# Five blocks of x loaded ahead instead of seven, and the last eight tiles scaled on GpSimd in a graph-attention kernel

## What is computed

```python
def reference(x, adj, key, value, Wq, bq, Wk, bk, Wv, bv, Wm, bm):
    q, k, v = x @ Wq.T + bq, key @ Wk.T + bk, value @ Wv.T + bv
    scores = einsum('nd,md->nm', q, k) / sqrt(4096) * adj
    scores = where(abs(scores) < 1e-5, -1e9, scores)
    y = x + einsum('nm,md->nd', softmax(scores), v) @ Wm.T + bm
    return (y - mean(y)) / sqrt(var(y) + 1e-5)        # over the last axis
```

## Time and profile before

| what | value |
|---|---|
| median of 3 runs | 447.91 us (447.75 to 448.69) |
| profiled execution, its own time | 449.37 us |
| its span, first to last instruction | 447.6 us |
| PE busy | 432.1 us (97%) |
| DVE busy | 315.8 us (71%) |
| ACT busy | 190.3 us (43%) |
| POOL busy | 168.7 us (38%) |
| mean granted PE clock | 0.990 of 2.4 GHz |
| DMA | 121.58 MB, 272 GB/s in the mean |

### The profile page before, as it was taken

The page is one execution under the profiler, slowest core; times in us unless marked ns, Lnnn a source line. Parts: engine busy times, 40 slices in busy tenths (PEclk is TensorE's granted clock), DMA queues, the critical chain, the costliest instruction groups (busy, mean ns, idle before and its releaser), DMA issues.

```text
span 447.6 us, 5475 instructions
## 1 busy us (share of the span) xinstructions
PE 432.1 (97%) x1536; PEld 245.7 (55%) x1536; DVE 315.8 (71%) x923; ACT 190.3 (43%) x448; POOL 168.7 (38%) x180
## 2 busy tenths in 40 slices
PE   8999999899999999999999999999999999999982
PEld 5344444344444456566666666666566656666651
DVE  0347525698439647787888889888879878847675
ACT  1233422323333243434445454554545445464573
POOL 3100000000425118463655656547205776174300
PEclk9999999989999999999999999999999999999997
DMA  8999999999999999987899999999949879568333
GB/s 324 369 236 276 294 287 288 227 244 240 284 321 331 343 307 257 299 306 234 252 299 261 325 317 326 339 346 304 299 169 302 256 227 364 168 187 292 108 142 115
DMA packets 32452, 121.58 MB, mean 272 GB/s; under 512 B 5080, under 2 KB 5336, under 8 KB 30370
## 3 DMA queue, kind: packets, MB, share of 16 engines
q0 software_dynamic: 16240, 72.79, 61.1%
q1 hardware_dynamic: 12866, 28.51, 17.6%
q10 hardware_dynamic: 3312, 19.89, 11.3%
HBM read 139.78 MB, written 17.56 MB: 352 GB/s over the span
## 4 chain that ended last, share of the span: by engine, by line
PE 76%; issue 10%; DMA 6%; DVE 4%; ACT 3%; POOL 1%; POOLq 0%; DVEq 0%; ACTq 0%
PE bank L574 24%; PE bank L564 14%; PE bank L682 12%; PE bank L720 12%; PE bank L664 6%; DMA big<-adj_tiles 6%; PE bank L615 3%; PE bank L693 2%; PE bank L673 2%; PE bank L608 1%; ACT keyT L893 1%; ACT y_buf L951 1%; DVE stats L1277 1%; POOL big L462 1%; DVE big L1057 1%
## 5 line engine op out<-in xcount | busy, mean ns | idle before, releaser
L574 PE MATMUL bank<-big,M 128*128 128x472 f32 (+1 forms) x288 | 121.9, 550 | 0.3 <-ACT y_buf L838 0.3
L564 PE MATMUL bank<-y_buf,big 128*128 128x512 f32 x256 | 113.3, 602 | 0.7 <-ACT y_buf L860 0.7
L481 POOL DMA_INDIRECT v_g<-table,index x70 | 71.9, 1027 | 80.8 <-PE bank L720 51.9
L471 POOL DMA_INDIRECT key_adj_g<-key_adj,index x70 | 73.3, 1046 | 49.7 <-DVE index L1145 29.0
L564 PEld LDWEIGHTS bank<-y_buf,big 128*128 128x128 f32 x256 | 48.7, 192 | 60.5 <-issue 59.0
L574 PEld LDWEIGHTS bank<-big,M 128*128 128x128 f32 x288 | 51.9, 190 | 46.0 <-issue 43.8
L1057 DVE TENSOR_TENSOR big<-big 128x1888 bf16<-128x1888 bf16 x35 | 39.8, 1137 | 52.9 <-DMA big<-adj_tiles 52.9
L682 PE MATMUL bank<-keyT,qT 128*118 128x256 f32 x280 | 66.3, 380 | 0.7 <-ACT keyT L893 0.7
L462 POOL DMA_DIRECT2D big<-adj_tiles x35 | 19.9, 568 | 124.5 <-PE bank L564 82.0
L720 PE MATMUL bank<-v_g,probT 128*118 128x512 f32 x136 | 64.0, 593 | 0.5 <-ACT probT L930 0.5
L682 PEld LDWEIGHTS bank<-keyT,qT 128*118 128x118 f32 x280 | 50.8, 182 | 22.6 <-issue 10.9
(11 more groups left out here) (122 smaller groups left out, 469.8 us busy)
## 6 DMA issues: line engine op xcount, KB each, us to landing
big<-adj_tiles POOLq DMA_DIRECT2D x35, 944.0 KB, 14.6
x_buf<-x SPq DMA_DIRECT2D x35, 256.0 KB, 7.4
out<-y_buf SPq DMA_DIRECT2D x34, 256.0 KB, 5.5
big<-valueT ACTq DMA_DIRECT2D x8, 1024.0 KB, 11.3
big<-xT SPq DMA_DIRECT2D x7, 944.0 KB, 10.6
table<-qT ACTq DMA_DIRECT2D x5, 1024.0 KB, 14.6
table<-y_buf ACTq DMA_DIRECT2D x3, 1024.0 KB, 16.0
big<-xT ACTq DMA_DIRECT2D x2, 944.0 KB, 8.6
```

Of the source, the lines that this page charges most:

```text
L471: pool.indirect_dma_start(key_adj_g[:, b, c, :], None, key_adj, bass.IndirectOffsetOnAxis(index[:, t, CH + c:CH + c + 1], 0),).then_inc(ke ...
L481: pool.indirect_dma_start(v_g[:, b, c, :], None, table, bass.IndirectOffsetOnAxis(index[:, t, c:c + 1], 0), bounds_check=N - 1, oob_is_err ...
L564: mm = nc.tensor.matmul(bank[4 + t % 2][:, :], col_buf[nb % 2][:, d, k * P:(k + 1) * P], G[:, d, :], start=(d == 0), stop=(d == DC - 1))
L574: mm = nc.tensor.matmul(ps[:, 0:n], M[:, d, a * P:(a + 1) * P], xT_buf[nb % 2][:, d, 0:n], start=(d == 0), stop=(d == DC - 1))
```

## The change

Five blocks of x are loaded ahead of the loop instead of seven; the other two follow inside the loop, behind the load of xT. Tiles 26 to 33 (`LATE`) are scaled by POOL, behind its last gather, instead of by ACT; their stores come last in SP's order. The roots of 31 and 32 (step 34) and of 33 (step 35) are refined by seven short operations each on POOL instead of four for all three on DVE. ACT takes the roots of 31 and 32 ahead of `copy_prob(34)`. The keys of tile 34 are copied in two parts with `sizes(33)` between them. `add_x(32)` moves behind the first operation of `soften(34)`. The four fillers before the last `prob_transposes` are removed.

```diff
+XAHEAD = 5
...
-            last = {T - 3: [T - 7, T - 6, T - 5], T - 1: [T - 4, T - 3, T - 2], T: [T - 1]}
+            last = {T - 3: [T - 7, T - 6, T - 5], T - 1: [T - 4, T - 3], T: [T - 2], T + 1: [T - 1]}
...
+        LATE = range(T - 9, T - 1)
...
-            if i == T:
-                return [T - 2, T - 1]
-            if i == T - 3:
-                return sqrt_of(i - 2)[2:]
-            if i >= T - 2:
-                ready = sqrt_of(T - 3)
-                return ready[:2] if i == T - 2 else ready[2:] + sqrt_of(i)[:2]
+            if i > T - 4:
+                return []
...
-            for t in range(XB):
+            for t in range(XAHEAD):
                 load_x(t)
...
-                if i >= 1 and i + XB - 1 < T:
-                    load_x(i + XB - 1)
-            store(T - 2)
+                if i + XAHEAD < T:
+                    load_x(i + XAHEAD)
+            for t in LATE:
+                store(t)
...
+            def finish(t):
+                y = y_buf[0:R, t % YB, :]
+                nc.gpsimd.tensor_scalar(y, y, rstd[0:R, t:t + 1], shift[0:R, t:t + 1], ALU.mult, ALU.add).then_inc(late_fin, 1)
+
+            def scales(i, ts):
+                a, b = ts[0], ts[-1] + 1
+                n = i - (T - 1)
+                near, step = std[0:R, a:b], shift[0:R, a:b]
+                pool.wait_ge(std_sb, roots_before(i) + 1)
+                nc.gpsimd.tensor_scalar(step, mean_var[0:R, a:b, 1], EPS, None, ALU.add).then_inc(late_step, 1)
+                pool.wait_ge(late_step, 4 * n + 1)
...
+                nc.gpsimd.tensor_tensor(rstd[0:R, a:b], step, near, ALU.mult).then_inc(late_rstd, 1)
...
+            for t in LATE:
+                if t < T - 4:
+                    pool.wait_ge(shift_sb, scaling_of(t))
+                if t in (T - 4, T - 2):
+                    i = T - 1 if t == T - 4 else T
+                    scales(i, sqrt_of(i))
+                finish(t)
...
-                if i == T - 1:
-                    keep_clock(4)
...
                 if i < T:
+                    if i == T - 2:
+                        copy_keys(i + 1, range(1))
                     sizes(i)
-                    if i == T - 1:
-                        finish(late.pop(0))
-                    if LAST_QUERY < i < T - 1:
+                    if i == T - 2:
+                        copy_keys(i + 1, range(1, CH))
+                    elif LAST_QUERY < i < T - 2:
                         copy_keys(i + 1)
...
-                if i < T - 1 and sqrt_of(i):
+                if sqrt_of(i):
                     roots(i, sqrt_of(i))
...
+            roots(T + 1, sqrt_of(T + 1))
+            finish_half(T - 1)
...
                 if t < T - 1:
                     key_bias(t + 1)
+                else:
+                    add_x(t - 2)
...
                 for t in values_of(i):
-                    add_x(t)
+                    if t != T - 3:
+                        add_x(t)
...
-                if sqrt_of(i):
+                if i < T - 1 and sqrt_of(i):
                     scales(i, sqrt_of(i))
                 if i == T:
+                    scales(T + 1, sqrt_of(T + 1))
```

More of the change, by code:

```diff
@@ L251, in build @@
         fin_sb = sem("fin_sb")
+        late_fin = sem("late_fin")
+        late_step = sem("late_step")
+        late_rstd = sem("late_rstd")
+        late_shift = sem("late_shift")
         last_sb = sem("last_sb")
@@ L376, in scaling_of @@
         def scaling_of(t):
-            return next(roots_before(i + 1) for i in range(T + 1) if t in sqrt_of(i))
+            return next(roots_before(i + 1) for i in range(T + 2) if t in sqrt_of(i))
         def scores_of(t):
@@ L416, in store @@
             def store(t):
-                sp.wait_ge(fin_sb, t + 1)
+                if t in LATE:
+                    sp.wait_ge(late_fin, LATE.index(t) + 1)
+                else:
+                    sp.wait_ge(fin_sb, t + 1)
                 sp.dma_start(out_tiles[t], y_buf[:, t % YB, :]).then_inc(stored[t % YB], 16)
@@ L524, in _ @@
                     gather_keys(i + KD)
+            def finish(t):
[8 more added lines that the diff above has]
+                pool.wait_ge(late_step, 4 * n + 1)
+                nc.gpsimd.tensor_tensor(step, step, near, ALU.mult).then_inc(late_step, 1)
+                pool.wait_ge(late_step, 4 * n + 2)
+                nc.gpsimd.tensor_tensor(step, step, near, ALU.mult).then_inc(late_step, 1)
+                pool.wait_ge(late_step, 4 * n + 3)
+                nc.gpsimd.tensor_scalar(step, step, -0.5, 1.5, ALU.mult, ALU.add).then_inc(late_step, 1)
+                pool.wait_ge(late_step, 4 * n + 4)
+                nc.gpsimd.tensor_tensor(rstd[0:R, a:b], step, near, ALU.mult).then_inc(late_rstd, 1)
+                pool.wait_ge(late_rstd, n + 1)
+                nc.gpsimd.tensor_tensor(step, mean_var[0:R, a:b, 0], rstd[0:R, a:b], ALU.mult).then_inc(late_shift, 1)
+                pool.wait_ge(late_shift, 2 * n + 1)
+                nc.gpsimd.tensor_scalar(step, step, -1.0, None, ALU.mult).then_inc(late_shift, 1)
+                pool.wait_ge(late_shift, 2 * n + 2)
+            for t in LATE:
[5 more added lines that the diff above has]
+                finish(t)
             with overflow(pool) as n:
@@ L886, in copy_q, with copy_keys @@
                                      ).then_inc(q_sb, 1)
-            def copy_keys(t):
+            def copy_keys(t, chunks=range(CH)):
                 if t >= 1:
@@ L891, in copy_keys @@
                 act.wait_ge(keyT_adjT_ps, t + 1)
-                for c in range(CH):
+                for c in chunks:
                     nc.scalar.activation(keyT[:, :, c * P:(c + 1) * P],
@@ L942, in finish_half @@
                 y = y_buf[0:R, t % YB, 0:HD]
-                act.wait_ge(shift_sb, scaling_of(t))
+                act.wait_ge(shift_sb, roots_before(T - 1) + 1)
                 nc.scalar.activation(y, y, ACT.Identity, bias=shift[0:R, t:t + 1], scale=rstd[0:R, t:t + 1]
                                      ).then_inc(fin_sb, 1)
-                act.wait_ge(fin_sb, T)
+                act.wait_ge(fin_sb, LATE[0] + 1)
                 act.dma_start(out_tiles[t][:, 0:HD], y_buf[:, t % YB, 0:HD]).then_inc(stored[t % YB], 16)
@@ L954, in _ @@
             for i in range(T + 1):
-                late = finish_of(i)
                 if i <= LAST_QUERY:
@@ L973, in _ @@
                     copy_q(u, bank[7])
[L974 to L980, removed]
+                for t in finish_of(i):
+                    finish(t)
+            roots(T + 1, sqrt_of(T + 1))
+            finish_half(T - 1)
             with overflow(act) as n:
@@ L1295, in scales @@
                 a, b = ts[0], ts[-1] + 1
-                n = roots_before(i)
+                n = roots_before(min(i, T - 1))
                 near, step = std[0:R, a:b], shift[0:R, a:b]
-                dve.wait_ge(std_sb, n + 1)
+                dve.wait_ge(std_sb, roots_before(i) + 1)
                 nc.vector.scalar_tensor_tensor(step, mean_var[0:R, a:b, 1], EPS, near, ALU.add, ALU.mult).then_inc(newton_sb, 1)
@@ L1337, in _ @@
                     shift_lists(b, 4, SHIFTS)
-                if sqrt_of(i):
+                if i < T - 1 and sqrt_of(i):
                     scales(i, sqrt_of(i))
                 if i == T:
+                    scales(T + 1, sqrt_of(T + 1))
+                if i == T:
                     y = y_buf[0:R, (T - 1) % YB, HD:D]
-                    dve.wait_ge(shift_sb, scaling_of(T - 1))
+                    dve.wait_ge(shift_sb, roots_before(T - 1) + 1)
                     nc.vector.tensor_scalar(y, y, rstd[0:R, T - 1:T], shift[0:R, T - 1:T], ALU.mult, ALU.add
```

## The result

The changed kernel takes 449.97 us in the median of 6 runs (449.32 to 450.73), the kernel before 447.88 us in 6 runs beside it (447.75 to 448.69): a ratio of 1.0044, 95% interval 1.0033 to 1.0056. It is slower by 0.44%; 443.5 us was forecast, and the range ended at 446.9. The profiled execution of the changed kernel took 450.3 us, its span is 448.5 us against 447.6 before.

The account below looks back on a forecast made before the run. PE, busy 97% of the span, was taken to bound the kernel, with long waits near 88 us and in the tail. 3.2 us (x) plus 1.2 us (tail) off 447.91 gave 443.5 us, range 441.9 to 446.9.

Parts of the forecast that it names:

- the GpSimd sum of the tail: Tail: from 435.9, fourteen short POOL operations and three scalings end at 442.4; last store issued about 442.75.
- the 3.2 us of x: Start: two x blocks fewer bring tile 9 1.5 us earlier, and the clock kept up saves 1.7 us more.
- the prediction's signs of being wrong: Unchanged wait near 88 us, DVE waiting over 6.2 us for tile 19, clock 0.50 under last values, POOL ending after 444.
- The prices of GpSimd's operations: Tail on POOL: 0.27 us for a short operation, 0.9 us for a scaling of 512 columns.
- the 1.2 us forecast: Tail: last store issued at about 442.75 us instead of 443.98, 1.2 us earlier.
- the front of the tail: Steps 33 and 34: splitting tile 34's key copy saves PE 0.3 us; DVE goes on 1.15 us earlier after absolute values.
- the 1.7 us for the clock: PE at 90 to 94 us: no clock fall after a 0.48 us wait, saving 1.7 us.
- GpSimd ends last by far: Rival, tail: scalings over 2.1 us, POOL ends at 449.3 if they take 2.6; slower, 450.4 us; chance 0.10.
- GpSimd and DVE hold each other up: Rival, step of scores 33: POOL's scalings delay DVE's two-operand SBUF operations, 1.3 us uncovered; 444.8 us; chance 0.10.
- fell neither early: Rival near 88 us: PE's wait shortens but the clock falls all the same; 445.2 us; chance 0.13.
- nor in the tail: Rival, tail: clock falls after 1.3 us idle without fillers, last values take 1.96 us more; 444.4 us; chance 0.10.

Follow-up runs that it names:

- x_only: The kernel before with only the x part: five blocks of x loaded ahead instead of seven; 446.57 us, ratio 0.9945.
- the eight traces against the four: Traces with five x blocks ahead (tile 9's tree starts at 83.76 to 84.49 us) against those with seven (85.29 to 85.59 us).
- early_drain: The changed kernel with one explicit GpSimd drain behind the last gather, ahead of the late scalings; 445.94 us, ratio 0.9926.
- drain_tail: The changed kernel with the x part undone and an explicit GpSimd drain behind the last gather; 446.80 us, ratio 0.9963.
- drain_best: The changed kernel plus early GpSimd drain, tiles 26 to 30 and 33 scaled on ScalarE, tile 33's short operations on VectorE; 444.80 us, ratio 0.9914.
- tail_only: The changed kernel with the x part undone, seven blocks of x ahead again; 451.41 us, ratio 1.0054.
- late_touch: The kernel before with one GpSimd memset of an unused column, waiting for the last half of the output; 454.56 us, ratio 1.0108.

## Why the prediction was wrong, point by point

**The step that failed is the GpSimd sum of the tail.** It ran "From 435.9: 1.9 + 1.8 + 1.9 + 0.9 = 442.4", took the last store's issue for the end and compared it with the last issue before. What stands behind GpSimd's last instruction was left out: a closing drain of 7.2 us. In the kernel before it lay under the loop's last steps, 423.6 to 431.5 us, so it cost nothing; moved behind 440.57 it ends 4 us after everything else. Its row was in the trace of before, under the line that closes the program, which the prediction leaves out. Priced from there, 7.2 us from the last gather's end or 7.9 for the whole row, and with the 0.4 us between scaling and drain that the changed kernel shows, the forecast's own tail would have read 450.0 to 450.7 us, that is 446.8 to 447.5 with the 3.2 us of x off, against a span of 447.6: at most 0.8 us of gain, and with the 1.3 us that x is worth at the median a loss of 1.1 to 1.8. None of the prediction's signs of being wrong came (POOL's last instruction ended at 440.57, not after 444): they, too, watched the work and not the close.

**The prices of GpSimd's operations were right.** The seven short operations begin 0.29 us apart in the mean (434.08 to 435.82 is 1.74 us for six steps; 0.27 was taken), a scaling takes 0.76 to 1.0 us (0.9 was taken), and GpSimd ends 0.55 us behind ScalarE's last half (440.57 and 440.02). From the last tile's product to the last store the tail went from 11.46 to 10.39 us, 1.07 us less; of the 1.2 us forecast 0.9 lay there. The other 0.3, the front of the tail, didn't come (see the rivals). The 769 ns of the Trainium skill's "GPSIMD Engine Reference", which the prediction had set beside its 0.9, agree with the 0.77 of the single scaling.

**x: right mechanism, size too large.** Tile 9 moved by 1.1 us here and 1.8 in x_only, and by 1.5 in the mean of the eight traces against the four, as forecast; the wait vanished, since PE also came 0.9 us later to it (the value products ahead of it start at 85.01 us instead of 84.10; why is open); the clock stayed up. By the profile that made 2.8 us at the loop's start. But the 1.7 us for the clock (1.8 by the four traces), right for the profiled execution, were subtracted from a median that stands among executions without them: the prediction kept the profiled execution's 1.46 us above the median as a constant, and that distance, as far as the mean clocks tell, was this very clock. At the median the x part is worth 1.3 us.

**The rivals.** Of the five, "GpSimd ends last by far" gave 450.4 us, close to what was measured, by another mechanism: it wanted scalings over 2.1 us, and they took 0.8. That GpSimd and DVE hold each other up came true, and the forecast's sum has nothing for it. First the changed kernel in step 32, where GpSimd scales tiles 26 and 27, then the kernel before:

```profile
419.50 0.47 DVE L1269 SCALAR_TENSOR_TENSOR score<-bank,c_cols,adjT 118x256 f32<-118x256 f32 x1
421.48 0.89 DVE L1278 CUSTOM_DVE_ANT_0 score<-score,size 118x256 f32<-118x256 f32 x1
422.02 1.75 POOL L534 TENSOR_SCALAR y_buf<-y_buf,rstd,shift 118x512 f32<-118x512 f32 x2
426.23 0.48 DVE L1269 SCALAR_TENSOR_TENSOR score<-bank,c_cols,adjT 118x256 f32<-118x256 f32 x1
```

```profile
421.91 0.48 DVE L1235 SCALAR_TENSOR_TENSOR score<-bank,c_cols,adjT 118x256 f32<-118x256 f32 x1
423.88 0.43 DVE L1242 CUSTOM_DVE_ANT_0 score<-score,size 118x256 f32<-118x256 f32 x1
428.17 0.48 DVE L1235 SCALAR_TENSOR_TENSOR score<-bank,c_cols,adjT 118x256 f32<-118x256 f32 x1
```

From the product of step 32 to that of step 33 it is 6.73 us instead of 6.26, and 6.26 again in early_drain, where GpSimd is still in its drain. In step 33 the two operations with both inputs in SBUF took 1.04 and 0.79 us, where they take 0.74 and 0.43 undisturbed, and from that product to the next it is 4.35 us as before, but 3.84 in early_drain. So in steps 32 and 33 together 1.0 us is lost on the path, of the 1.3 that the rival allowed in one step, more than the 0.5 us that the front of the tail saves, and with the 1.07 behind the last product the tail gains only 0.6 us in this kernel's trace, against 1.2 forecast (from the product of step 32 to the last store 21.47 us for 22.07). The Trainium skill's "SBUF — State Buffer", section "Who interferes with whom", calls this an exclusive lock; here no operation lost a whole scaling, each became 0.28 to 0.46 us longer, and one with a single tensor input did too (0.60 for 0.32 us in early_drain). The clock fell neither early nor in the tail, after an idle time of 1.33 us there.

**The sum as the runs give it**, from the undisturbed 447.86: minus 1.3 for x, minus 1.1 for the tail, plus 4.0 for the exposed drain (449.97 - 445.94) makes 449.5; 449.97 was measured. The 1.1 is that of drain_tail, whose scalings run in other steps; with the 0.6 us of the changed kernel's own tail and the 3.9 us behind its last store, an estimate from two traces, it is 449.9.

## What to carry to other kernels

An engine's last instruction isn't its end: before work is put late on an engine that has been quiet, look in the trace of before at what closes that engine and how long it takes, above all where it issued gathers, and if it is long, have it done earlier by a drain of one's own under other work. A term read from one profiled execution belongs in a forecast of the median only if the other runs show it; their mean clocks tell, within one kernel. (Between kernels they mislead: the changed kernel's six runs read 0.990 to 0.993, though its trace has 1.00 up to 440 us and 0.52 in the idle end behind.) And operations put on GpSimd have to be priced with what they do to VectorE's beside them. Before a third engine is given the work of two busy ones, count the room inside their own waits: in drain_best ScalarE and VectorE did it better.

## What the runs showed of the hardware

- GpSimd's drain: 0.11 us with no gather since the last drain, 0.28 with 2, 5.60 with 64, 7.23 to 7.25 with 140, the last 20 us after the last gather too. Placed right behind gathers its row is 7.9 to 9.2 us long and begins under the last of them; from their end it is 7.0 to 7.2 us, and 14.9 of a row of 18.8 in the middle of the loop. In the same closing lines of the changed kernel VectorE's takes 57 ns and ScalarE's 81. The Trainium skill's "VectorE: DVE Perf Modes", section "The DRAIN you can't avoid", gives about 12 ns for the drains with which a program opens and closes, on all five engines; on GpSimd behind gathers the measurement decides, and it is some 600 times that.
- The clock: after PE's idle times of 1.33 us (tail of the changed kernel) and 1.5 us (near 88 us in tail_only, 1.00 from 90 to 94 us) it stayed at its upper level; after 1.98 us (before, 0.57) and 2.1 us (late_touch, 0.61) it was mostly at 1.2 GHz from 90 to 94 us.
